# Local attention scores issued in three parts, with the halves of the next key projection between them

## The chip, the cores and the metric

The kernel runs on one core of a Trainium2 chip. The metric is the device time of one execution in microseconds (us). The core has a matrix engine (TensorE, PE in the profile, with its weight loads shown apart as PEld), VectorE (DVE), ScalarE (ACT), GpSimd (POOL) and SyncE (SP), which here issues the DMAs. Each engine works through its own list of instructions in order; semaphores hold an instruction back until work of another engine is done.

## The reference, cut to what matters

The input x is (2, 1024, 128). The result is x plus a causal attention (8 heads, 2 latent key/value groups) plus the output of a stack of six layers, both applied to the layer-normed x. Each of the six layers is a local attention with 16 heads of width 64 and windows of 32 tokens, and then a gated feed-forward part:

```python
x = attn_layer(shift_tokens(x), Wqkv[i], q_scale[i], k_scale[i], Wo[i]) + x
x = ffn_layer(shift_tokens(x), ln_g[i], ln_b[i], W1[i], b1[i], W2[i], b2[i]) + x
# inside attn_layer: q, k l2-normalised, scaled, rotated by position; then for each window of 32 queries
sim  = jnp.einsum('bhwie,bhwje->bhwij', bq, bk2) * QK_SCALE   # 32 queries x 64 keys (the window before and its own)
sim  = jnp.where(mask, -jnp.finfo(sim.dtype).max, sim)
attn = jax.nn.softmax(sim, -1)
out  = jnp.einsum('bhwij,bhwje->bhwie', attn, bv2)
```

The change touches only where the products of `sim` stand in the matrix engine's list.

## The kernel before, in words

The first 250 us or so are the causal attention. Then comes one long software pipeline over 96 tiles of 128 tokens (6 layers x 16 tiles), one step G per tile, about 15 us each. No loop runs on the chip: everything is unrolled, and each engine has its own hand-written order of calls for a step. A tile k passes through the steps as follows.

- Step G = k: TensorE projects the keys of tile k (`project_keys`, `projected`, L1205, six 128x512 products into banks 0 and 1, three for each half of the heads). ScalarE squares them (`square_keys`, L767), VectorE multiplies them by the cosine and the sine tables (`cosine_keys` L1061, `sine_keys` L1066), and GpSimd adds the two parts (L548). At the end of step k+1 TensorE transposes the keys (`transpose_keys`, L1443).
- Step k+1: TensorE projects the queries into the same banks 0 and 1 (`project_queries`, L1205). It may do so only when `sine_keys` has read the keys out of them, which is the semaphore k_s.
- Step k+2: TensorE computes the values (`values_lower`, `values_upper`, L1494) into banks 4 and 5, ScalarE copies them out (L807) and then writes the mask into the same banks (`mask_scores`, L822). The scores (`scores`, L1479) are added onto the mask: 8 head pairs x 4 windows x 2 heads are 64 small products in the program, 128 matmul records in the trace, since each 32-bit product shows as two. The last one raises s_mm.
- s_mm is waited for by VectorE, which takes the row maxima (`maxima`, L1113) and subtracts them (`subtract`, L1119, which raises s_sub), and by GpSimd, which copies the last window of keys for the next tile (`lookback`, L570). The subtraction frees banks 4 and 5 for `values_lower` of the next step. ScalarE takes the exponentials (L840).
- Later steps: denominators (L1101, L1103), scaling on GpSimd (L543), transposes of the probabilities (L1443), the weighted sum (`weigh`, L1518), and once in four tiles the feed-forward products (L1205 again) with their gelus (L873).

The order of TensorE around the change is, in one step: `weigh`, `values_lower`, `project_queries`, the column transpose of the normed rows (L1536), `transpose_queries`, `values_upper`, some feed-forward products, `transpose_probs`, more of these, `scores`, `project_keys`, `transpose_keys`. VectorE's order is: `sum_queries` (L1095), `cosine_queries`, `sine_queries`, `normalise_rows` (L1128), `maxima`, `subtract`, `cosine_keys`, (once a layer the lower part of W1, L1143), `sine_keys`, `sum_keys` (L1089), `attended` (L1108), `denominators`. In GpSimd's order `scale_keys` (L602) and `lookback` (L570) stand ahead of `rotate_queries` (L553), `scale_queries` (L608) and `rotate_keys` (L548).

Of the kernel before, what the change touches and what calls it, by code (L numbers as in the profile page):

```python
# [33 lines left out]
DEPTH, LH, LD, WIN = 6, 16, 64, 32  # L34
HALF = LD // 2
HD = LH * LD
NP = LH // 2
NW = P // WIN
# [60 lines left out]
def build(nc, x, wqT, wkd4, wvd, wkuT, wvuT, wo, wqk, wvo, w1, w2, par, sca, cst_d, tab_d, out):  # L99
    ctx = ExitStack()  # L100
    with ctx:
# [94 lines left out]
        def bk(i):  # L196
            return banks[:, 512 * i:512 * i + 512]
# [41 lines left out]
        def is_tile(G):  # L239
            return 0 <= G <= LAST_TILE  # L240
# [962 lines left out]
        def _(pe):  # L1203
# [78 lines left out]
                ins.then_inc(s["b1_mm"], 1)  # L1282
                freed[7] = ("b1", l + 1)

            def projected(k, z):

                b, i = tile_at(k)
                xH, xL = xsH[:, b, P * i:P * (i + 1)], xsL[:, b, P * i:P * (i + 1)]
                claim(0, 1)
                for h in range(2):  # L1290
                    c0, c1 = 512 * h, 512 * (h + 1)
                    mm(bk(h), xH, qkH[:, z, c0:c1], True, False)
                    mm(bk(h), xH, qkL[:, z, c0:c1], False, False)
                    ins = mm(bk(h), xL, qkH[:, z, c0:c1], False, True)
                return ins

            def project_keys(k):
                if is_tile(k):
                    pe.wait_ge(s["xs_L"], k // 4 + 1)
                    pe.wait_ge(s["wk_L"], k // TILES + 1)  # L1300
                    projected(k, 0).then_inc(s["k_mm"], 1)
                    freed[0] = freed[1] = ("k_s", k + 1)

            def score_row(o, it, h, i):
# [162 lines left out]
                    transposes(prob[:, k % 2, :]).then_inc(s["pt_mm"], 1)  # L1467
                    freed[2] = freed[3] = ("pt_cp", k + 1)

            def scores(k):  # L1470
                if is_tile(k):
                    pe.wait_ge(s["kT_cp"], k + 1)
                    pe.wait_ge(s["qT_cp"], k + 1)
                    pe.wait_ge(s["s_msk"], k + 1)
                    for j in range(NP):
                        for w in range(NW):
                            for o in range(2):
                                r = slice(64 * o, 64 * o + 64)
                                ins = pe.matmul(bk(4 + o)[WIN * w:WIN * (w + 1), 64 * j:64 * (j + 1)],  # L1479
                                                qT[r, j, WIN * w:WIN * (w + 1)], kT[r, j, WIN * w:WIN * w + 64],  # L1480
                                                start=False, stop=True, skip_group_check=True)
                    ins.then_inc(s["s_mm"], 1)
                    freed[4] = freed[5] = ("s_sub", k + 1)

            def values(k, g):

# [99 lines left out]
            for G in range(STEPS):  # L1586
                if G == 1:
                    shifts(0)
                weigh(G - 4)
                values_lower(G - 2)  # L1590
                project_queries(G - 1)
                ln_columns(G - 6)
                transpose_queries(G - 2)
                values_upper(G - 2)
                up_gate(chunk_at(G, 10), 0)
                up_gate(chunk_at(G, 10), 1)
                up_value(chunk_at(G, 11), 0)
                up_value(chunk_at(G, 12), 1)
                next_products_lower(G - 2)
                down(chunk_at(G, 13))  # L1600
                transpose_probs(G - 3)
                up_value(chunk_at(G, 12), 2)
                up_gate(chunk_at(G, 11), 2)
                scores(G - 2)
                next_products_upper(G - 2)
                if G:
                    project_keys(G)
                next_shifts(chunk_at(G, 12))
                layer_columns(chunk_at(G, 13))
                transpose_keys(G - 1)  # L1610
# [55 lines left out]
```

## Time and profile before

| | |
|---|---|
| median of 3 runs | 1748.52 us (1745.69 to 1751.39) |
| the profiled execution | 1745.55 us |
| its span | 1743.9 us, 72603 instructions |
| busy share | PE 93%, DVE 86%, POOL 77%, ACT 76% |
| TensorE's mean granted clock | 0.984 |
| the 95 intervals from the first scores to the last | 252.5 to about 1696 us, 15.2 us each |

The profile's page gives shares over the whole span. TensorE is the busiest engine, yet four engines are all busy for more than three quarters of the time, so that what counts is which wait ends last at each place of a step. The timeline shows this: each row is one instruction or a run of equal ones, with its start, its length, its engine and line, and in square brackets the time that the engine sat idle before it and what ended this. "issue" there is idle time in which the engine waited for nothing that the profile shows. A name such as "banks<-arena" says what is written and read; the local names kT, qT, kc and so on are all parts of the buffer `arena`.

### The profile page before, as it was taken

Reading aid. Unit: us, or ns where it says so; the run is one execution under the profiler, and the core shown is the slowest. Engines: PE = TensorE matmul, PEld = TensorE weight load, DVE = VectorE, ACT = ScalarE, POOL = GpSimd, SP = SyncE. Lnnn points to the kernel's source line nnn. Section 1 sums busy time; section 2 is a strip of 40 time slices with the busy share of each in tenths; the row PEclk is TensorE's granted clock in tenths of the full one; section 3 lists DMA queues with packets and bytes.
Section 4 is the critical chain, followed back from the end, with each engine's and each line's share of the span. In section 5 each row is a group of like instructions: output and inputs, shape, how many; then the busy total and the mean of one; then the engine's idle time right before and its main releaser. Section 6 shows DMA issues by size and latency. Waiting matters only on the chain.

```text
span 1743.9 us, 72603 instructions
## 1 busy us (share of the span) xinstructions
PE 1619.5 (93%) x31192; PEld 1098.7 (63%) x31192; DVE 1495.5 (86%) x1863; ACT 1318.4 (76%) x1934; POOL 1340.6 (77%) x1311
## 2 busy tenths in 40 slices
PE   6999978889999999999998999999999999999995
PEld 4777855556566666665665666666666666666654
DVE  5677857999889998898998888999999988999982
ACT  3788846687787788778777877877887887788773
POOL 2312159888988899988888888899888998888871
PEclk8999989999999999999999999999999999999997
DMA  5221100100001000011000010000010000000001
GB/s 158 67 50 39 38 1 30 35 7 8 15 7 59 6 8 12 16 31 34 8 12 14 8 57 7 7 12 15 7 59 7 12 6 15 8 7 7 8 7 28
DMA packets 47997, 40.61 MB, mean 23 GB/s; under 512 B 33216, under 2 KB 41152, under 8 KB 46016
## 3 DMA queue, kind: packets, MB, share of 16 engines
q1 hardware_dynamic: 47680, 35.98, 7.4%
q8 instruction: 249, 4.08, 0.9%
q14 instruction: 68, 0.56, 0.1%
HBM read 20.22 MB, written 1.05 MB: 12 GB/s over the span
## 4 chain that ended last, share of the span: by engine, by line
PE 51%; DVE 22%; issue 13%; ACT 8%; POOL 6%; DMA 0%; SPq 0%; DVEq 0%; POOLq 0%; ACTq 0%
PE banks L1205 23%; PE banks L1494 9%; PE banks L1443 5%; PE banks L1518 4%; DVE arena L1066 4%; PE banks L1479 4%; PE banks L1335 4%; DVE lnx L1128 3%; DVE small L1095 3%; DVE small L1101 2%; DVE small L1089 2%; DVE small L1113 2%; DVE arena L1061 2%; ACT arena L807 1%; ACT L873 1%
## 5 line engine op out<-in xcount | busy, mean ns | idle before, releaser
L1494 PE MATMUL banks<-M,xs 128*32 128x512 f32 x3072 | 368.0, 596 | 0.6 <-ACT arena L807 0.3
L1061 DVE TENSOR_TENSOR arena<-banks,tabs 128x1024 f32<-128x1024 f32 x192 | 233.8, 1218 | 35.5 <-ACT arena L767 22.4
L548 POOL TENSOR_TENSOR arena<-arena 128x1024 f32<-128x1024 f32 x96 | 229.8, 2393 | 43.7 <-DVE arena L1066 43.3
L807 ACT ACTIVATE arena<-banks 128x1024 f32<-128x1024 f32 x192 | 197.0, 1026 | 68.3 <-PE banks L1494 67.6
L1066 DVE TENSOR_TENSOR arena<-banks,tabs 128x1024 f32<-128x1024 f32 x192 | 233.2, 1215 | 0.0
L553 POOL TENSOR_TENSOR arena<-arena 128x1024 f32<-128x1024 f32 x96 | 228.3, 2378 | 0.0
L543 POOL TENSOR_TENSOR prob<-prob,small 128x1024 f32<-128x1024 f32 x96 | 184.0, 1916 | 30.0 <-DVE small L1103 30.0
L1128 DVE SCALAR_TENSOR_TENSOR lnx<-lns,small 128x128 f32<-128x128 f32 x96 | 175.3, 1826 | 34.2 <-POOL small L596 32.8
L1205 PE MATMUL banks<-qkH,xsH 128*128 128x512 f32 x384 | 173.1, 451 | 32.1 <-DVE arena L1066 29.2
L1518 PE MATMUL banks<-arena 128*32 128x128 f32 x6144 | 190.9, 277 | 5.6 <-ACT arena L873 4.2
L608 POOL TENSOR_TENSOR arena<-arena,small 128x1024 f32<-128x1024 f32 x96 | 182.9, 1906 | 9.8 <-POOL arena L553 0.4
L602 POOL TENSOR_TENSOR arena<-arena,small 128x1024 f32<-128x1024 f32 x96 | 182.9, 1905 | 7.5
L767 ACT ACTIVATE arena<-banks 128x1024 f32<-128x1024 f32 x96 | 98.3, 1024 | 113.6 <-PE banks L1205 113.4
L1479 PE MATMUL banks<-arena 64*32 64x64 f32 x12288 | 147.2, 226 | 32.0 <-issue 17.0
L1518 PEld LDWEIGHTS banks<-arena 128*32 128x32 f32 x6144 | 164.5, 111 | 12.4 <-issue 6.0
L1479 PEld LDWEIGHTS banks<-arena 64*32 64x32 f32 x12288 | 130.1, 105 | 58.4 <-issue 56.8
L1494 PEld LDWEIGHTS banks<-M,xs 128*32 128x32 f32 x3072 | 88.4, 110 | 123.2 <-issue 116.2
L1205 PEld LDWEIGHTS banks<-qkH,xsH 128*128 128x128 f32 x384 | 73.2, 191 | 132.8 <-issue 110.0
L1205 PE MATMUL banks<-qkL,xsH 128*128 128x512 f32 x384 | 153.6, 400 | 2.4 <-issue 2.4
L1205 PE MATMUL banks<-qkH,xsL 128*128 128x512 f32 x384 | 153.7, 400 | 0.0
L778 ACT ACTIVATE arena<-banks 128x1024 f32<-128x1024 f32 x96 | 98.4, 1025 | 72.0 <-PE banks L1205 71.8
L1443 PEld LDWEIGHTS banks<-cst,arena 64*128 64x128 f32 x3072 | 111.5, 139 | 61.8 <-issue 41.9
(134 smaller groups left out, 3645.4 us busy)
## 6 DMA issues: line engine op xcount, KB each, us to landing
qkraw<-in_wqk_dram SPq DMA_DIRECT2D x6, 1024.0 KB, 5.2
arena<-in_wvo_dram SPq DMA_DIRECT2D x5, 1024.0 KB, 5.4
gq<-w1w SPq DMA_DIRECT2D x64, 64.0 KB, 2.0
lns<-Xt SPq DMA_DIRECT2D x96, 32.0 KB
lns<-Xt SPq DMA_DIRECT2D x96, 31.8 KB
xsH<-w1w SPq DMA_DIRECT2D x32, 64.0 KB, 2.0
xsL<-w1w SPq DMA_DIRECT2D x32, 64.0 KB, 2.0
W<-in_w_dram SPq DMA_DIRECT2D x6, 341.0 KB, 3.2
```

The source lines that it names most:

```text
L543: pool.tensor_tensor(p, p, d, ALU.mult).then_inc(s["p_nrm"], 1)
L548: pool.tensor_tensor(kc, kc, ks, ALU.add).then_inc(s["k_add"], 1)
L553: pool.tensor_tensor(qc, qc, qs, ALU.add).then_inc(s["q_add"], 1)
L807: act.activation(vw[:, (2 * k + g) % RV, :], two(V_BANK), ACT.Copy).then_inc(s[f"v_cp{g}"], 1)
L1061: dve.tensor_tensor(heads(c), heads(two(0)), table(k % NT, kind), ALU.mult).then_inc(s[done], 1)
L1066: dve.tensor_tensor(w.rearrange("p (h z k) -> p h z k", h=LH, z=2), swapped(two(0)), table2(k % NT, kind + 1), ALU.mult).then_inc(s[done], 1)
L1128: dve.scalar_tensor_tensor(lnx[:, :], lns[:, k % 2, :], ag[:, k % 2, 0:1], rs[:, 4, 32:33].to_broadcast([P, D]), ALU.subtract, ALU.mult).t ...
L1205: return pe.matmul(o, l, r, start=start, stop=stop)
L1443: ins = pe.transpose(bk(2 + o)[:, 64 * k:64 * (k + 1)], src[r, P * k:P * (k + 1)], ident[r, r])
L1479: ins = pe.matmul(bk(4 + o)[WIN * w:WIN * (w + 1), 64 * j:64 * (j + 1)], qT[r, j, WIN * w:WIN * (w + 1)], kT[r, j, WIN * w:WIN * w + 64], ...
L1494: ins = pe.matmul(bk(V_BANK + z)[WIN * q:WIN * (q + 1), :], xs[:, b, t0:t0 + WIN], M[:, q, :, :].rearrange("p m n -> p (m n)"), start=True ...
L1518: ins = pe.matmul(bk(PV_BANK)[WIN * w:WIN * (w + 1), 0:D], ptile[:, NQ * z + m, WIN * w:WIN * (w + 1)], block_of(k, w - 1 + z)[:, D * m:D ...
```

## The change

The 64 products of `scores` are issued in three parts of 24, 24 and 16 (head pairs 0 to 2, 3 to 5, and 6 and 7). The first three products of `project_keys` stand between the first and the second part, the last three between the second and the third. Where there is no key projection (the last two tiles) the parts stand one after another. The waits ahead of the scores stand ahead of the first part; s_mm is raised by the last product of the third part. `next_products_upper`, which has work once a layer, now stands behind the third part. The operands, the results and all other engines' instructions are the same.

```diff
-            def projected(k, z):
+            def projected(k, z, between=None):
                 ...
                 for h in range(2):
+                    if h and between:
+                        between()
                     c0, c1 = 512 * h, 512 * (h + 1)
                     mm(bk(h), xH, qkH[:, z, c0:c1], True, False)
                     mm(bk(h), xH, qkL[:, z, c0:c1], False, False)
                     ins = mm(bk(h), xL, qkH[:, z, c0:c1], False, True)
...
-                    projected(k, 0).then_inc(s["k_mm"], 1)
+                    projected(k, 0, (lambda: scores_middle(k - 2)) if k >= 2 else None).then_inc(s["k_mm"], 1)
...
+            def scored(k, pairs):
+
+                for j in pairs:
+                    for w in range(NW):
+                        for o in range(2):
+                            r = slice(64 * o, 64 * o + 64)
+                            ins = pe.matmul(bk(4 + o)[WIN * w:WIN * (w + 1), 64 * j:64 * (j + 1)],
+                                            qT[r, j, WIN * w:WIN * (w + 1)], kT[r, j, WIN * w:WIN * w + 64],
+                                            start=False, stop=True, skip_group_check=True)
+                return ins
+
+            def scores_first(k):
                 if is_tile(k):
                     pe.wait_ge(s["kT_cp"], k + 1)
                     pe.wait_ge(s["qT_cp"], k + 1)
                     pe.wait_ge(s["s_msk"], k + 1)
-                    for j in range(NP):
-                        ...
-                    ins.then_inc(s["s_mm"], 1)
+                    scored(k, range(0, 3))
                     freed[4] = freed[5] = ("s_sub", k + 1)
+
+            def scores_middle(k):
+                if is_tile(k):
+                    scored(k, range(3, 6))
+
+            def scores_last(k):
+                if is_tile(k):
+                    if not is_tile(k + 2):
+                        scores_middle(k)
+                    scored(k, range(6, NP)).then_inc(s["s_mm"], 1)
...
-                scores(G - 2)
-                next_products_upper(G - 2)
+                scores_first(G - 2)
                 if G:
                     project_keys(G)
+                scores_last(G - 2)
+                next_products_upper(G - 2)
```

TensorE's list before, from the scores of a tile to the next query projection (L1479 scores, L1205 key projection, L1443 transposes of the keys, L1518 weighted sum, L1494 values, and L1205 at the end the queries; in brackets the semaphores that a row waits for):

```order
L1479 MATMUL banks<-arena 32x64 [waits s_msk,qT_cp,kT_cp]
L1479 MATMUL banks<-arena 32x64 x63
L1205 MATMUL banks<-qkH,xsH 128x512 [waits q_s,wk_L,xs_L]
L1205 MATMUL banks<-qkL,xsH 128x512
L1205 MATMUL banks<-qkH,xsL 128x512
L1205 MATMUL banks<-qkH,xsH 128x512
L1205 MATMUL banks<-qkL,xsH 128x512
L1205 MATMUL banks<-qkH,xsL 128x512
L1443 MATMUL banks<-cst,arena 128x64 [waits pt_cp,k_nrm]
L1443 MATMUL banks<-cst,arena 128x64 x15
```

The same place of the changed kernel's list, where the scores have line L1478 and the transposes L1445:

```order
L1478 MATMUL banks<-arena 32x64 [waits s_msk,qT_cp,kT_cp]
L1478 MATMUL banks<-arena 32x64 x23
L1205 MATMUL banks<-qkH,xsH 128x512 [waits q_s,wk_L,xs_L]
L1205 MATMUL banks<-qkL,xsH 128x512
L1205 MATMUL banks<-qkH,xsL 128x512
L1478 MATMUL banks<-arena 32x64 x24
L1205 MATMUL banks<-qkH,xsH 128x512
L1205 MATMUL banks<-qkL,xsH 128x512
L1205 MATMUL banks<-qkH,xsL 128x512
L1478 MATMUL banks<-arena 32x64 x16
L1445 MATMUL banks<-cst,arena 128x64 [waits pt_cp,k_nrm]
L1445 MATMUL banks<-cst,arena 128x64 x15
```

The last product of the scores stood ahead of all six products of the key projection, and now stands behind all six. The last product of the key projection stood behind 64 products of the scores, and now stands behind 48. VectorE's list around the wait for s_mm is the same in both kernels:

```order
L1128 SCALAR_TENSOR_TENSOR lnx<-lns,small 128x128 [waits lnB_mm,rk]
L1113 TENSOR_REDUCE small<-banks 128x16 [waits s_mm]
L1119 TENSOR_TENSOR prob<-banks,small 128x1024 [waits s_max,pt_mm]
L1061 TENSOR_TENSOR arena<-banks,tabs 128x1024 [waits kT_mm,k_sq,tab]
L1066 TENSOR_TENSOR arena<-banks,tabs 128x1024 [waits k_add,k_sq]
```

The fourth and fifth rows are the cosine and sine products of the keys; they stand behind the row that waits for s_mm.

## Rows read from the trace of the kernel before

**Rows 1.** The profile's page: busy time, and the chain that ended last, by engine.
```profile
PE 1619.5 (93%) x31192; PEld 1098.7 (63%) x31192; DVE 1495.5 (86%) x1863; ACT 1318.4 (76%) x1934; POOL 1340.6 (77%) x1311
...
PE 51%; DVE 22%; issue 13%; ACT 8%; POOL 6%; DMA 0%; SPq 0%; DVEq 0%; POOLq 0%; ACTq 0%
```

**Rows 2.** Waits of TensorE, 260 to 1700 us: total, times, longest, in us.
```profile
PE banks L1205 <- DVE arena L1066: 23.5, 50, 1.8
PE banks L1479 <- issue: 17.0, 14, 2.6
```

**Rows 3.** Waits of VectorE, 260 to 1700 us: total, times, longest, in us.
```profile
DVE small L1113 <- PE banks L1479: 11.5, 11, 2.0
```

**Rows 4.** Timeline of one step, all engines: start, length (us), engine, line, work.
```profile
1261.91 1.47 PE L1479 MATMUL banks<-arena 64*32 64x64 f32 x128
...
1263.32 0.50 PE L1205 MATMUL banks<-qkH,xsH 128*128 128x512 f32 x1
...
1263.65 0.39 PE L1205 MATMUL banks<-qkL,xsH 128*128 128x512 f32 x1
...
1264.43 0.46 POOL L570 COPY arena<-arena 128x256 f32<-128x256 f32 x1
...
1264.56 1.21 DVE L1113 TENSOR_REDUCE small<-banks 128x16 f32<-128x1024 f32 x1
...
1264.90 0.72 PE L1443 MATMUL banks<-cst,arena 64*128 64x64 f32 x16
1265.01 1.03 ACT L767 ACTIVATE arena<-banks 128x1024 f32<-128x1024 f32 x1 [1.92 <-PE banks L1205]
...
1265.87 1.23 DVE L1119 TENSOR_TENSOR prob<-banks,small 128x1024 f32<-128x1024 f32 x1
1267.01 1.22 DVE L1061 TENSOR_TENSOR arena<-banks,tabs 128x1024 f32<-128x1024 f32 x1
...
1267.33 1.93 PE L1494 MATMUL banks<-M,xs 128*32 128x512 f32 x16
...
1267.38 1.90 POOL L608 TENSOR_TENSOR arena<-arena,small 128x1024 f32<-128x1024 f32 x1
...
1268.14 1.22 DVE L1066 TENSOR_TENSOR arena<-banks,tabs 128x1024 f32<-128x1024 f32 x1
...
1269.51 0.47 PE L1205 MATMUL banks<-qkH,xsH 128*128 128x512 f32 x1 [0.25 <-DVE arena L1066]
```

**Rows 5.** The profile's page: the group of all score products (busy, mean ns of one).
```profile
L1479 PE MATMUL banks<-arena 64*32 64x64 f32 x12288 | 147.2, 226 | 32.0 <-issue 17.0
```

**Rows 6.** Timeline of TensorE: scores and the query projection of the next step.
```profile
1277.21 1.48 PE L1479 MATMUL banks<-arena 64*32 64x64 f32 x128
...
1284.90 0.51 PE L1205 MATMUL banks<-qkH,xsH 128*128 128x512 f32 x1
...
1291.55 1.47 PE L1479 MATMUL banks<-arena 64*32 64x64 f32 x128
```

**Rows 7.** Timeline of TensorE: the first and the last of 53 short steps.
```profile
298.57 1.47 PE L1479 MATMUL banks<-arena 64*32 64x64 f32 x128 [1.46 <-ACT banks L822]
...
306.16 0.47 PE L1205 MATMUL banks<-qkH,xsH 128*128 128x512 f32 x1 [0.27 <-DVE arena L1066]
...
1653.23 1.47 PE L1479 MATMUL banks<-arena 64*32 64x64 f32 x128
...
1660.82 0.47 PE L1205 MATMUL banks<-qkH,xsH 128*128 128x512 f32 x1
```

**Rows 8.** Timeline of VectorE: the step in which the lower part of W1 is made.
```profile
1342.81 1.55 DVE L1143 SCALAR_TENSOR_TENSOR w1w<-W,parv,w1w 128x682 fp32r<-128x682 f32 x1
```

**Rows 9.** Timeline of TensorE: scores that stood still in the middle.
```profile
1045.12 0.99 PE L1479 MATMUL banks<-arena 64*32 64x64 f32 x76
1048.73 1.06 PE L1479 MATMUL banks<-arena 64*32 64x64 f32 x52 [2.62 <-issue]
1049.73 0.79 PE L1205 MATMUL banks<-qkH,xsH 128*128 128x512 f32 x1
```

**Rows 10.** The profile's page: the queue that brings instructions (packets, MB, share).
```profile
q8 instruction: 249, 4.08, 0.9%
```

More of the change, by code:

```diff
@@ L1468, in transpose_probs @@
                     freed[2] = freed[3] = ("pt_cp", k + 1)
-            def scores(k):
+            def scored(k, pairs):
[8 more added lines that the diff above has]
+            def scores_first(k):
                 if is_tile(k):
@@ L1474, in scores @@
                     pe.wait_ge(s["s_msk"], k + 1)
-                    for j in range(NP):
[L1476 to L1481, printed above, removed]
-                    ins.then_inc(s["s_mm"], 1)
-                    freed[4] = freed[5] = ("s_sub", k + 1)
+                    scored(k, range(0, 3))
+                    freed[4] = freed[5] = ("s_sub", k + 1)
+            def scores_middle(k):
[6 more added lines that the diff above has]
+                    scored(k, range(6, NP)).then_inc(s["s_mm"], 1)
             def values(k, g):
```

## The prediction, made before the changed kernel had run

> **What bounds the kernel now.** I read the page first. TensorE is busy for 93% of the span and VectorE for 86%, and the chain that ended last spends 51% on TensorE, 22% on VectorE and 13% in time without a visible wait [rows 1]. So TensorE is close to the bound, and part of every step goes through VectorE. Next I read the lists of waits, to see at which places one engine waits for the other. From 260 to 1700 us TensorE waits 50 times, 23.5 us in all, for VectorE's sine product of the keys (L1066) before it projects the queries, and stands still 14 times, 17.0 us in all, in the middle of the scores for nothing that the profile shows [rows 2]. In the other direction VectorE waits for the scores in 11 steps only, 11.5 us in all [rows 3].
>
> Then the timeline of one step, which shows how these two belong together [rows 4]. The reader should follow two paths from the start of the scores, S = 1261.91, to the start of the query projection, Q = 1269.51, and count from S:
> - TensorE's own path: scores, key projection from 1.41, transposes from 2.99, weighted sum, values from 5.42, and Q at 7.60. It has 0.25 us of idle time before Q.
> - VectorE's path: after the normalising of rows (L1128) the maxima start at 2.65, the subtraction at 3.96, the cosine at 5.10, the sine at 6.23, which ends at 7.45, and 0.15 us later Q starts.
> Both paths end together, within a quarter of a microsecond. The scores end at 1.47, and VectorE comes to the maxima only at 2.65: it is 1.18 us late, so that s_mm is not what it waits for. From the start of the maxima to Q it needs 1269.51 - 1264.56 = 4.95 us, with nothing idle in it.
>
> **What the change does to s_mm and k_mm.** It removes and adds no work. First the price of going from scores to a projection. One record of the scores lasts 0.226 us [rows 5], and all of them 1.47, so the last one starts 1.25 after S; the first key product starts at 1.41 [rows 4], 0.16 later. The second starts 0.33 after the first, where the rest follow at (1264.90 - 1263.65)/5 = 0.25 or a little less [rows 4]. So the passage costs about 0.16 + 0.08 = 0.24 us, taken as 0.25. The change makes this passage twice a step instead of once. The trace shows no passage in the middle of a projection, so the bounds are 0 (the weights of the second half are loaded under the scores) and 0.5 (the passage back costs as much again). I take 0.25, by the one passage that the rows show.
> The transposes then start at 2.99 + 0.25 = 3.24, and the last product of the scores stands just ahead of them. It starts a little before, at 3.16 (between 0.01 and 0.16 before, by the spacing of two scores, 1.25/127, and by the passage above), and with its 0.226 ends at 3.38. s_mm is thus late by 3.38 - 1.47 = 1.91 us. k_mm comes only about 0.1 us earlier than before: 32 of the 128 records are no longer ahead of it (32 x 1.47/128 = 0.37), and one more passage (0.25) is. That gives nothing in an ordinary step, because ScalarE's square of the keys starts at 3.10 and is over at 4.13, while the cosine product that waits for it starts at 5.10 [rows 4].
>
> **What stands behind the late s_mm.** VectorE holds four operations behind this wait: maxima, subtraction, cosine, sine. They begin at 3.38 and a few hundredths for the semaphore, say 3.42, instead of 2.65, and Q comes at 3.42 + 4.95 = 8.37; I take 8.40. TensorE's own path would bring it there at 7.35 + 0.25 = 7.60, so it now waits for VectorE, partly before the values (banks 4 and 5 are free when the subtraction ends, at 3.42 + 1265.87 + 1.23 - 1264.56 = 5.96, and TensorE comes there at 5.42 + 0.25 = 5.67) and partly before the queries. From Q to the next S everything hangs on Q (projection, square, copy of the transposed queries, upper values, their copy, the mask) and I leave it unchanged. GpSimd waits for s_mm too, with the copy L570, which comes at 2.52 now and at 3.42 then; the queue behind it is two long operations (L553, L608), which end at 1269.28, 4.85 us after its start. So GpSimd reaches the next addition of keys at 8.27, just when the sine product is over (8.25). That cover is used up to the last tenth. If it falls short, GpSimd's later work comes 0.1 to 0.2 us later in a step, up to 15 us in all, which the range holds.
>
> **The sum.** I read S and Q of 93 steps in TensorE's timeline. In 53 of them Q - S is below 7.86, with a mean of 7.66 (7.59 in the first and the last [rows 7], 7.60 in the example [rows 4], 7.69 in the one behind it [rows 6]). Each of them goes to 8.40:
> - 53 x (8.40 - 7.66) = +39 us.
> - Six steps, one in each layer, have the lower part of W1 (1.55 us, L1143) between the cosine and the sine [rows 8]. It becomes part of the same path: they go from about 8.3 (once 9.2) to about 9.85, +8.5 us.
> - 13 steps in which the scores stand still, or the clock falls after it, have Q - S from 8.3 to 11.4 now. If the standstill goes they take 8.4: -12 us.
> - The other 21 steps are long already for other reasons (a standstill elsewhere, the first and last steps of a layer) and hide the delay: -1 to 0 us.
> - Some standstills stay: +4 us.
> Together about +39 us, to which the last steps, outside the 93, add 1.
>
> **The standstills.** In one step 76 of the records run, then TensorE stands for 2.62 us, and the key product behind it takes 0.79 us [rows 9] instead of 0.50 [rows 4]. Instructions come by a queue of their own, 249 packets with 4.08 MB, 16.4 KB each [rows 10]. Nearly all instructions are TensorE's 2 x 31192 loads and products [rows 1]; 4.08 MB over these are 65 bytes each, so a packet holds about 250 of them, an estimate. One packet takes 0.9% of 16 engines' 1744 us over 249, which is 1.0 us. The scores are 128 loads and 128 products, a packet in 1.47 us, the fastest stretch of the step. My estimate is that the next packet can't come in that time, and that with a projection half (0.95 us) after each 96 instructions it can. Bounds: all 17.0 us go, and with them some 5 us by which the products behind the longest ones are stretched (an estimate: 0.29 us on each of some 17 products), so -22, or none, 0. I take -12 + 4 = -8 net, since part of the gain would be hidden under the longer path, nearer to the first because the standstills lie in the fastest burst.
> The Trainium skill, page "Runtime: NRT & Kernel Launch", section "Instruction fetch mechanics", says that instructions come in blocks of 256 and that their fetch is hidden because the sequencer issues more slowly than the blocks arrive. The block size agrees with the trace; by the second part the standstills have another cause and stay, which is rival B. The 17.0 us that stand in the trace speak against it here.
>
> The profiled execution took 1745.6 us, so the same with the change is 1785.6. The median of the runs is 3.0 above the profiled one, and I predict 1788.
>
> **Rivals.**
> - A, the forecast: s_mm is late by 1.9 us, VectorE's four operations set Q. 1765 to 1808. Chance 0.72. Its lower part is a passage cost of 0: Q at 8.15, -0.25 x 75 = -19 us, 1769.
> - B, the same with standstills that stay where they are (or go into the projection halves): 1788 + 20 = 1808, up to 1815. For it: some stand next to 1 MB loads of weights, which splitting doesn't move. Against it: most don't. Chance 0.17.
> - C, the delay of s_mm is hidden: VectorE comes to the maxima 1.2 us late anyway, and if its path has slack that I don't see, TensorE's own sum remains: two passages, +0.25 x 93 = +23, and -22. 1749. For it: TensorE is the busiest engine. Against it: 50 waits for L1066 in the trace, so no slack. Chance 0.05.
> - D, faster: the place is the score burst, the mechanism is the instruction supply. The standstills go with their low clock, -22 us, the passages cost nothing, and VectorE's late arrival hides s_mm. 1727. It decides if Q - S stays at 7.7. The 0.25 us of idle time before Q, with VectorE as the reason [rows 4], speak against it. Chance 0.06.
>
> A difference of under 0.3% (5 us) can't be told from none here. Slower by more: A and B, 0.89, and I take 0.01 off for their edge: 0.88. Same: C and that edge, 0.06. Faster: D, 0.06. The range for 8 in 10 is A with its bounds and the start of B: 1764 to 1811.
>
> **What would show it.** Right: VectorE's wait for the scores (now L1478) rises from 11 times to nearly all 96, about 100 us in all; the maxima start within 0.1 us of the last score; Q - S is 8.3 to 8.5 in ordinary steps; TensorE waits for the subtraction (L1119) before the values, which it never did, and for L1066 before the queries in most steps; the standstills in L1478 fall well below 17 us. The step from 1261.91 to 1277.21, 15.3 us long [rows 4, 6], would take 16.1. Wrong: if Q - S stays at 7.7 (C or D), if the maxima don't start at s_mm, or if the first product of the second half starts more than 0.3 us or less than 0.1 us after the middle scores.

## The result: 4.5% slower, twice the predicted loss

The changed kernel takes 1831.07 us (median of 6 runs, 1825.78 to 1832.87); the kernel before took 1752.19 in the runs beside it (6 runs, 1745.69 to 1757.31). The ratio is 1.045, with a 95% interval from 1.0425 to 1.0476. The forecast was 1788 in a range of 1764 to 1811: slower was right, the size was not. The profiled execution has a span of 1831.2 us, 87.3 more than the 1743.9 before.

The page of the changed kernel, first the busy times (us and share of the span), then the chain that ended last:

```profile
PE 1685.6 (92%) x31192; PEld 1100.6 (60%) x31192; DVE 1500.1 (82%) x1863; ACT 1327.9 (73%) x1934; POOL 1339.3 (73%) x1311
...
PE 58%; DVE 21%; issue 13%; ACT 5%; POOL 2%; DMA 0%; DVEq 0%; SPq 0%; ACTq 0%; POOLq 0%
```

VectorE, ScalarE and GpSimd do the same work in nearly the same time as before [rows 1] in a longer span. TensorE is shown busy for 66 us more with the same instructions. More than half of that is the scores, whose group has 183.8 us on this page and 147.2 on the page before [rows 5]: the three parts of a step count 0.71 + 0.72 + 0.45 = 1.88 us, the whole counted 1.47. The waits say where the rest of the longer span went. TensorE's, from 260 to 1785 us (total, times, longest):

```profile
PE banks L1205 <- DVE arena L1066: 35.0, 74, 2.1
PE banks L1510 <- DVE prob L1119: 20.7, 63, 2.1
...
PE banks L1445 <- POOL prob L543: 6.4, 11, 0.8
PE banks L1478 <- issue: 3.4, 4, 1.9
PE banks L1445 <- ACT M L826: 3.1, 5, 0.6
```

The wait for the sine product of the keys grew from 50 times and 23.5 us [rows 2]; the wait of the values (L1510) for the subtraction is new; the standstills in the scores fell from 14 and 17.0 us [rows 2] to 4 and 3.4. VectorE's wait for the scores, and then GpSimd's:

```profile
DVE small L1113 <- PE banks L1478: 121.0, 93, 4.0
```

```profile
POOL arena L570 <- PE banks L1478: 108.9, 81, 3.2
POOL arena L567 <- PE banks L1478: 21.9, 11, 2.2
```

VectorE waited for the scores in 11 steps before [rows 3], and now in 93. One ordinary step of the changed kernel, which answers to [rows 4] (start, length, engine, line, work, and in brackets the idle time before it):

```profile
1354.02 0.71 PE L1478 MATMUL banks<-arena 64*32 64x64 f32 x48 [0.15 <-ACT banks L822]
...
1354.63 2.10 DVE L1128 SCALAR_TENSOR_TENSOR lnx<-lns,small 128x128 f32<-128x128 f32 x1 [0.70 <-POOL small L596]
...
1354.66 0.50 PE L1205 MATMUL banks<-qkH,xsH 128*128 128x512 f32 x1
1354.68 1.91 POOL L602 TENSOR_TENSOR arena<-arena,small 128x1024 f32<-128x1024 f32 x1
...
1355.23 0.40 PE L1205 MATMUL banks<-qkH,xsL 128*128 128x512 f32 x1
1355.56 0.72 PE L1478 MATMUL banks<-arena 64*32 64x64 f32 x48
1356.21 0.50 PE L1205 MATMUL banks<-qkH,xsH 128*128 128x512 f32 x1
...
1357.11 0.45 PE L1478 MATMUL banks<-arena 64*32 64x64 f32 x32
...
1357.49 0.71 PE L1445 MATMUL banks<-cst,arena 64*128 64x64 f32 x16
1357.69 1.23 DVE L1113 TENSOR_REDUCE small<-banks 128x16 f32<-128x1024 f32 x1 [0.96 <-PE banks L1478]
1357.72 0.40 POOL L570 COPY arena<-arena 128x256 f32<-128x256 f32 x1 [1.14 <-PE banks L1478]
...
1359.02 1.23 DVE L1119 TENSOR_TENSOR prob<-banks,small 128x1024 f32<-128x1024 f32 x1
1360.16 1.22 DVE L1061 TENSOR_TENSOR arena<-banks,tabs 128x1024 f32<-128x1024 f32 x1
...
1360.39 1.92 PE L1510 MATMUL banks<-M,xs 128*32 128x512 f32 x16 [0.30 <-DVE prob L1119]
...
1361.29 1.22 DVE L1066 TENSOR_TENSOR arena<-banks,tabs 128x1024 f32<-128x1024 f32 x1
...
1362.65 0.47 PE L1205 MATMUL banks<-qkH,xsH 128*128 128x512 f32 x1 [0.34 <-DVE arena L1066]
```

Counted from S = 1354.02, the scores end at 3.54, the maxima start at 3.67, and Q, the start of the query projection, comes at 8.63. Before it was 1.47, 2.65 and 7.60. Both engines, VectorE and GpSimd, stand before the same semaphore for a microsecond.

The rows of L1128 and L602 show something that was overlooked when the slack at the maxima was read: what makes VectorE late there. The normalising row (L1128) is small. Its last four executions in the kernel before, with nothing of GpSimd beside them, take 0.34 to 0.35 us, and it takes 2.1 us here, beside GpSimd's scaling of the keys (L602). In 91 of its 96 executions, in this kernel as in the one before, it lasts 0.14 to 0.19 us longer than its overlap with L602. In the step of [rows 4] this scaling also ends where the maxima start:

```profile
1262.58 1.91 POOL L602 TENSOR_TENSOR arena<-arena,small 128x1024 f32<-128x1024 f32 x1
1263.09 1.55 DVE L1128 SCALAR_TENSOR_TENSOR lnx<-lns,small 128x128 f32<-128x128 f32 x1
```

The slack of 1.18 us thus hung on the place of L602 in GpSimd's list. No run moved L602, so what that would do to the time is not shown.

### The profile page after: what moved, and what is told of

Read it like the earlier page. It is cut to its first block, busy times and chain, and to the rows that moved or that the text cites. A ratio compares the mean times of both kernels' runs of the same rounds, so it can differ in the third digit from the quotient of the medians.

```text
span 1831.2 us, 72603 instructions
## 1 busy us (share of the span) xinstructions
PE 1685.6 (92%) x31192; PEld 1100.6 (60%) x31192; DVE 1500.1 (82%) x1863; ACT 1327.9 (73%) x1934; POOL 1339.3 (73%) x1311
## 4 chain that ended last, share of the span: by engine, by line
PE 58%; DVE 21%; issue 13%; ACT 5%; POOL 2%; DMA 0%; DVEq 0%; SPq 0%; ACTq 0%; POOLq 0%
PE banks L1205 30%; PE banks L1478 9%; PE banks L1510 8%; DVE small L1113 5%; DVE arena L1066 5%; PE banks L1445 4%; PE banks L1337 4%; DVE arena L1061 2%; ACT arena L807 2%; PE banks L1534 2%; ACT banks L822 2%; DVE small L1101 2%; DVE small L1089 2%; DVE arena L1152 1%; DVE prob L1119 1%
## 5 line engine op out<-in xcount | busy, mean ns | idle before, releaser
L1510 PE MATMUL banks<-M,xs 128*32 128x512 f32 x3072 | 371.4, 600 | 21.3 <-DVE prob L1119 20.7
L548 POOL TENSOR_TENSOR arena<-arena 128x1024 f32<-128x1024 f32 x96 | 229.9, 2395 | 21.7 <-DVE arena L1066 18.1
L1066 DVE TENSOR_TENSOR arena<-banks,tabs 128x1024 f32<-128x1024 f32 x192 | 233.2, 1215 | 0.0
L1205 PE MATMUL banks<-qkH,xsH 128*128 128x512 f32 x384 | 182.0, 474 | 44.3 <-DVE arena L1066 40.8
L1113 DVE TENSOR_REDUCE small<-banks 128x16 f32<-128x1024 f32 x96 | 117.6, 1225 | 126.6 <-PE banks L1478 126.6
L1128 DVE SCALAR_TENSOR_TENSOR lnx<-lns,small 128x128 f32<-128x128 f32 x96 | 175.2, 1825 | 38.9 <-POOL small L596 38.6
L1478 PEld LDWEIGHTS banks<-arena 64*32 64x32 f32 x12288 | 138.1, 106 | 111.8 <-issue 110.3
L543 POOL TENSOR_TENSOR prob<-prob,small 128x1024 f32<-128x1024 f32 x96 | 184.1, 1917 | 28.8 <-DVE small L1103 28.8
L1478 PE MATMUL banks<-arena 64*32 64x64 f32 x12288 | 183.8, 224 | 18.2 <-ACT banks L822 12.1
L608 POOL TENSOR_TENSOR arena<-arena,small 128x1024 f32<-128x1024 f32 x96 | 183.0, 1906 | 9.8 <-POOL arena L553 0.4
L602 POOL TENSOR_TENSOR arena<-arena,small 128x1024 f32<-128x1024 f32 x96 | 182.9, 1905 | 7.5
L1510 PEld LDWEIGHTS banks<-M,xs 128*32 128x32 f32 x3072 | 89.0, 110 | 156.4 <-issue 148.6
L840 ACT ACTIVATE prob<-prob 128x1024 f32<-128x1024 f32 x96 | 101.6, 1058 | 95.8 <-DVE prob L1119 95.5
L767 ACT ACTIVATE arena<-banks 128x1024 f32<-128x1024 f32 x96 | 98.3, 1024 | 97.9 <-PE banks L1205 97.5
L1205 PEld LDWEIGHTS banks<-qkH,xsH 128*128 128x128 f32 x384 | 72.9, 190 | 151.3 <-issue 124.2
L1205 PE MATMUL banks<-qkH,xsL 128*128 128x512 f32 x384 | 154.9, 404 | 0.0
```

The source lines that it names most:

```text
L543: pool.tensor_tensor(p, p, d, ALU.mult).then_inc(s["p_nrm"], 1)
L548: pool.tensor_tensor(kc, kc, ks, ALU.add).then_inc(s["k_add"], 1)
L608: pool.tensor_tensor(heads(qc), heads(qc), over(rs[:, 4, LH:2 * LH], LD), ALU.mult).then_inc(s["q_nrm"], 1)
L1066: dve.tensor_tensor(w.rearrange("p (h z k) -> p h z k", h=LH, z=2), swapped(two(0)), table2(k % NT, kind + 1), ALU.mult).then_inc(s[done], 1)
L1113: dve.reduce_max(nmax[:, :], two(4).rearrange("p (h k) -> p h k", h=LH), AXX).then_inc(s["s_max"], 1)
L1205: return pe.matmul(o, l, r, start=start, stop=stop)
```

## The experiments

Each time is a median; each ratio is to the kernel before, timed beside it on the same chip, and has its 95% interval.

### Is it the late semaphore or the added passages?

`keys_first` gives the key projection whole and then the scores whole: s_mm is late, but nothing is split.

```diff
-                scores(G - 2)
-                next_products_upper(G - 2)
                 if G:
                     project_keys(G)
+                scores(G - 2)
+                next_products_upper(G - 2)
```

> The kernel before with one edit: all six key products ahead of all 64 score products, nothing split. s_mm is late by a whole projection, but there is no passage back into a projection. Theory 1 (the late s_mm holds VectorE's four operations, and they set the start Q of the query projection): the scores end 3.1 to 3.3 us after the block of the two begins, Q comes 4.9 to 5.1 us after that, as in the changed kernel, and the time is 1795 to 1820 us. The scores stand whole, so their standstills come back: 10 us or more of unexplained idle time in the scores from 260 us to the end. Theory 2 (not the lateness but the two added passages between scores and projection cost the time): no passage is added, so it is within 5 us of the kernel before, about 1752.

Measured: 1803.27 us, ratio 1.0288 [1.0272, 1.0303]. Theory 1 holds, theory 2 falls: 51 of the 79 us of loss come with the late s_mm alone. In this kernel's timeline:

```profile
1312.57 0.50 PE L1205 MATMUL banks<-qkH,xsH 128*128 128x512 f32 x1
...
1314.16 1.48 PE L1479 MATMUL banks<-arena 64*32 64x64 f32 x128
...
1315.68 1.22 DVE L1113 TENSOR_REDUCE small<-banks 128x16 f32<-128x1024 f32 x1 [1.47 <-PE banks L1479]
```

The scores end 3.07 us after the block of the two begins, in place of 3.54. Of the standstills only 6.8 us (10 times, 260 to 1700 us) came back in the scores, less than expected; 15.4 us (26 times) of the same kind now stood in the weighted sum (L1518), which follows the scores closely here. So these gaps move with the list.

`last_before_half` keeps both passages, but raises s_mm before the last three key products. As a change to the changed kernel:

```diff
             def scores_middle(k):
                 if is_tile(k):
-                    scored(k, range(3, 6))
+                    scored(k, range(3, NP)).then_inc(s["s_mm"], 1)
...
                     if not is_tile(k + 2):
                         scores_middle(k)
-                    scored(k, range(6, NP)).then_inc(s["s_mm"], 1)
```

> The changed kernel with one edit: the third part of the scores follows the second at once and raises s_mm, ahead of the last three key products. Both passages stay, s_mm comes about 0.8 to 1.0 us earlier than in the changed kernel. Theory 1: Q comes 7.8 to 7.9 us after the start of the scores in place of 8.65, and the time falls by about 70 us, to 1755 to 1770. Theory 2 (passages): nothing is gained, 1820 to 1831. The standstills in the scores stay below 8 us by both.

Measured: 1763.19 us, ratio 1.0063 [1.0044, 1.0082]. Theory 1 again: 68 us come back for s_mm 0.96 us earlier. One of its steps:

```profile
1306.85 0.71 PE L1478 MATMUL banks<-arena 64*32 64x64 f32 x48
...
1308.39 1.04 PE L1478 MATMUL banks<-arena 64*32 64x64 f32 x80
1309.36 0.49 PE L1205 MATMUL banks<-qkH,xsH 128*128 128x512 f32 x1
...
1310.26 0.71 PE L1445 MATMUL banks<-cst,arena 64*128 64x64 f32 x16
...
1314.50 0.50 PE L1205 MATMUL banks<-qkH,xsH 128*128 128x512 f32 x1
```

The scores end 2.58 after S, about when VectorE comes to the maxima (2.65 in [rows 4]), and Q comes at 7.65. VectorE's wait for the scores is not all gone: 48 times, 43.7 us in all. The standstills missed: 13.9 us (14 times), not below 8.

With these two there are four kernels that differ in the time at which the scores end. Means over the same 53 ordinary steps, counted from the start of the first score or key product of the block, from the traces:

| kernel | scores end | Q |
|---|---|---|
| before | 1.51 | 7.66 |
| `last_before_half` | 2.63 | 7.86 |
| `keys_first` | 3.11 | 8.20 |
| changed | 3.59 | 8.68 |

The first 1.12 us of delay cost 0.20, since VectorE came late anyway; the next 0.96 cost 0.82.

### Is VectorE's path critical, and since when?

The maxima are taken over a query's own window of 32 keys, half of the elements, in the changed kernel and in the kernel before:

```diff
-dve.reduce_max(nmax[:, :], two(4).rearrange("p (h k) -> p h k", h=LH), AXX).then_inc(s["s_max"], 1)
+dve.reduce_max(nmax[:, :], two(4).rearrange("p (h k) -> p h k", h=LH)[:, :, WIN:2 * WIN], AXX).then_inc(s["s_max"], 1)
```

> The changed kernel, with the row maxima taken over the 32 keys of a query's own window alone (half of the elements are left out of the maximum, not of the softmax). The operation should take some 0.6 us in place of 1.21 and is the first of the four that wait for the scores. Theory 1: each step loses that time in full, 93 x 0.55 = 50 us less, 1775 to 1790. Theory 2 (TensorE's own work sets the step): under 10 us less, above 1820.

> The kernel before with the same half of the maxima left out. Here TensorE's own path ends within 0.25 to 0.4 us of VectorE's, so by theory 1 at most the 23.5 us can go that TensorE waits for the sine product of the keys: 1728 to 1745, a gain of less than half of that in the changed kernel. Theory 2: no change, 1748 to 1755. If the gain is as large as in the changed kernel, VectorE's path set the step before the change as much as after it, and both are wrong on what the change did.

Measured: on the changed kernel 1798.66 us, ratio 1.026 [1.0232, 1.0288], which is 32 us less than with the full maxima. On the kernel before 1750.37 us, ratio 0.9986 [0.9967, 1.0005], no difference that can be told. The same 0.53 us (692 ns for 1225, by the row of L1113) is worth 32 us in one kernel and, by the interval, 6 us at most in the other. So VectorE's path sets the step in the changed kernel, and it hardly did in the kernel before, where it ended level with TensorE's own: there Q - S falls in 26 steps, mostly from 7.59 to 7.23, 8.6 us in all, and TensorE waits for L1066 24 times in place of 50. In the profiled execution longer standstills in the scores (22.3 us for 17.0) and other steps take this back. Both sizes missed: 50 and 7 to 24 us were expected. On the changed kernel part of the rest is seen in the waits:

```profile
PE banks L1205 <- DVE arena L1066: 39.1, 68, 2.6
PE banks L1445 <- POOL prob L543: 19.2, 32, 1.0
```

With VectorE shorter, TensorE waits 19.2 us for GpSimd's scaled probabilities, where it was 6.4 with the full maxima. And the six steps with the row of W1 gain nothing before Q (10.4 us in both), for a reason that comes out two sections below.

### GpSimd's queue behind the same semaphore

GpSimd's copy of the last key window (`lookback`, L570) waits for s_mm. In this experiment it stands behind the addition of the queries, which needs nothing of it:

```diff
-                lookback(G - 1)
                 rotate_queries(G - 1)
+                lookback(G - 1)
```

> The changed kernel, with GpSimd's copy of the last key window (L570, which waits for s_mm) behind the addition of the rotated queries (L553) in its list, in place of ahead of it. Theory G (GpSimd's own queue behind s_mm is a second path of nearly the same length as VectorE's, and costs where GpSimd has extra work in a step): the steps lose the extra 1.0 us between Q and the next S that five of them have, and a few tenths elsewhere, so 1818 to 1828. Theory V (VectorE's path alone): no change, 1828 to 1833.

> The changed kernel with the maxima over half of the elements (half are left out of the maximum) and with GpSimd's copy behind L553. With the short maxima alone only 32 us went where 0.53 us x 93 = 49 were expected, and TensorE then waited 31 times, 18.5 us in all, for GpSimd's scaled probabilities (L543). Theory G: these 17 us come out now, 1779 to 1788. Theory V: something else holds them, 1794 to 1800, no change against the short maxima alone.

Measured: 1810.54 us on the changed kernel, ratio 1.0345 [1.0311, 1.0379], 20.5 us less. With the short maxima as well 1774.02 us, ratio 1.013 [1.0095, 1.0164], 24.6 us less than with these alone. The waits of the second kernel:

```profile
PE banks L1205 <- DVE arena L1066: 23.8, 64, 1.3
...
PE banks L1445 <- POOL prob L543: 4.0, 8, 0.8
```

Theory G holds and was too small: both results are below its range. The time from Q to the next S, summed over 93 steps of the timeline, was 653.7 us in the kernel before, 665.4 in the changed one and 653.4 with the late copy. The forecast had left this stretch unchanged. Nearly all of the 11.7 us stands in nine steps. In five of them, one ahead of each new layer, GpSimd also makes the next layer's key weights (L472, 2.39 us) behind the wait, and TensorE then waits for its scaled probabilities (L543): 5.2 us. In four it is the low clock behind the row of W1: 5.9 us. The L441 (1.30 us) of the step shown above costs nothing there: from Q to the next S it has 7.06 us in both kernels.

The same move on the kernel before:

> The kernel before with GpSimd's copy behind L553 alone. Theory G: GpSimd comes to the copy 1.0 us after the scores have ended, so nothing waits there, and the move frees nothing: within 5 us of 1752. A gain of 20 us as in the changed kernel would say that the place of the copy costs by itself, and not by the late s_mm.

Measured: 1750.23 us, ratio 1.0 [0.9983, 1.0017]. There, in an ordinary step, the copy comes 1.0 us after the scores have ended and waits for nothing (L570 waited for the scores 8 times in all, 8.9 us). It is the late s_mm that made its place cost 20 us.

### The row of W1 and the clock

VectorE makes the lower part of W1 once a layer (L1143), between the cosine and the sine of the keys. Here it stands behind the sine.

```diff
-                next_w1_lower(ahead_at(G, 13))
                 if G:
                     sine_keys(G)
+                next_w1_lower(ahead_at(G, 13))
```

> The changed kernel, with VectorE's lower part of W1 (L1143, 1.86 us, once a layer) behind the sine product of the keys in place of ahead of it. Theory C (in these six steps TensorE stands for 2.1 us ahead of the queries, and in four of them its clock then goes to 1.2 GHz for 3.4 us, which makes the next stretch 1.45 us longer): 6 x 1.8 + 4 x 1.45 = 16 us less, 1811 to 1819, and the low clock in these stretches is gone. Without the clock's part it would be 11 us, 1820. If the W1 row isn't on the path at all: 1831.

Measured: 1819.72 us, ratio 1.0389 [1.036, 1.0418], 11.4 us less. In the changed kernel's timeline of such a step (GpSimd and VectorE, then TensorE):

```profile
1149.02 1.90 POOL L608 TENSOR_TENSOR arena<-arena,small 128x1024 f32<-128x1024 f32 x1
1149.79 1.86 DVE L1143 SCALAR_TENSOR_TENSOR w1w<-W,parv,w1w 128x682 fp32r<-128x682 f32 x1
```

```profile
1152.93 0.47 PE L1205 MATMUL banks<-qkH,xsH 128*128 128x512 f32 x1 [2.04 <-DVE arena L1066]
...
1155.48 1.12 PE L1445 MATMUL banks<-cst,arena 64*128 64x64 f32 x16
1156.53 2.08 PE L1510 MATMUL banks<-M,xs 128*32 128x512 f32 x16
```

TensorE was idle for 2.04 us, and then its 16 transposes took 1.12 us in place of 0.71. The stretches before, in and after this (busy times, the granted clock as a share of 2.4 GHz, DMA share, GB/s) show the clock at 1.2 GHz for most of the middle one:

```profile
1148.90:1152.90 4.00, 1.98 (x28) 0.48 (x17) 4.00 (x4) 2.98 (x3) 1.94 (x2) 1.00 0.00 0
1152.90:1156.90 4.00, 3.97 (x27) 2.80 (x31) 3.54 (x8) 1.53 (x4) 3.65 (x2) 0.57 0.03 7
1156.90:1160.90 4.00, 3.96 (x38) 1.87 (x30) 3.01 (x3) 2.89 (x4) 2.05 (x6) 1.00 0.04 9
```

In four of the six such steps the time from Q to the next S grew by 1.45 to 1.48 us; in the other two TensorE was idle for as long (2.05 and 2.10 us), the clock stayed at 2.4 GHz and nothing was lost there. With the row moved, the clock is not at 1.2 GHz behind Q in any of the six, and Q - S falls by 1.7 to 1.8 us in each. But the time from Q to the next S is then 0.72 to 0.80 us longer in all six than in the kernel before, since the moved row delays the sums behind it, and GpSimd's L548 beside it takes 3.00 us in place of 2.39. The expectation had not counted this. The time of 1819.72 lies just above its range of 1811 to 1819 and is the 1820 that it gave for no part of the clock; the trace shows that the clock's part (5.9 us) was there and that the new delay (4.4 us) nearly made up for it.

The row itself takes 0.92 us in its new place and 1.86 in its old one. What it stands beside decides: in the kernel before, 0.82 us of GpSimd's L608 run beside it and it takes 1.54 or 1.55 in four of six cases; in the changed kernel 1.14 and it takes 1.86; with the short maxima it comes earlier, 1.68 run beside it and it takes 2.40, which is why these steps gained nothing. The short maxima first, then the late copy, where L608 is over before the row begins:

```profile
1125.43 1.91 POOL L608 TENSOR_TENSOR arena<-arena,small 128x1024 f32<-128x1024 f32 x1
1125.65 2.40 DVE L1143 SCALAR_TENSOR_TENSOR w1w<-W,parv,w1w 128x682 fp32r<-128x682 f32 x1
```

```profile
1136.46 1.90 POOL L608 TENSOR_TENSOR arena<-arena,small 128x1024 f32<-128x1024 f32 x1
...
1139.65 0.92 DVE L1143 SCALAR_TENSOR_TENSOR w1w<-W,parv,w1w 128x682 fp32r<-128x682 f32 x1
```

Both moves together on the changed kernel:

> The changed kernel with both list moves. Alone they gave 20.5 and 11.4 us. If they are two separate costs, 1799; if the stretch of low clock behind the W1 row was already freed by GpSimd's earlier copy (6 us counted twice), 1803 to 1807. What is then left over the kernel before, 48 to 56 us, is VectorE's path behind the late s_mm alone (Q 8.65 us after the start of the scores in an ordinary step). If less than 40 us were left, GpSimd's part would be larger than these moves show.

Measured: 1810.62 us, ratio 1.0331 [1.0286, 1.0375]. That is what the late copy alone gave (1810.54), above both expected ranges. The traces say why. The six W1 steps, from S to the next S, stand 17.8 us above the kernel before in the changed kernel, 7.7 with the late copy, 5.7 with the row moved and 5.6 with both. So the late copy alone had freed them of 10 us: with L608 out of the way the row takes 0.92 us, TensorE is idle for 1.1 to 1.2 us in place of 2.04, and the clock stays at 2.4 GHz. Some 2 us were left for the second move, less than can be told here. Half of what the late copy gave was the cost of the W1 row, of which the expectation had seen only the clock's 6 us as counted twice.

### Two tries for a faster kernel

`before_norm_late` moves VectorE's normalising of rows in the kernel before:

```diff
-                normalise_rows(G - 5)
                 maxima(G - 2)
...
                 attended(G - 3)
+                normalise_rows(G - 5)
                 denominators(G - 2)
```

> The kernel before, with VectorE's normalising of rows (L1128) moved from ahead of the maxima to behind the key sums and the attended rows. Theory 1: this row is what VectorE does while the scores run, and what makes it 1.2 us late at the maxima; with it gone s_mm is waited for at once, the four operations start 0.5 to 1.1 us earlier, and TensorE's own path sets Q at 7.35: the waits for L1066 (23.5 us) mostly go, 1730 to 1745. Rival: the moved row delays the denominators and GpSimd's scaling of the probabilities by 1 to 2 us, and TensorE waits there instead: 1752 to 1775.

Measured: 1804.19 us, ratio 1.0304 [1.0272, 1.0337]. It is slower, as the rival had it, but far above its 1752 to 1775, and in the main by another wait than it named:

```profile
PE banks L1536 <- DVE lnx L1128: 48.0, 57, 1.8
PE banks L1205 <- DVE arena L1066: 16.7, 25, 1.7
...
PE banks L1443 <- POOL prob L543: 9.5, 21, 1.5
```

TensorE's column transpose (L1536), which stands right behind the query projection, waits 48.0 us for the moved row. Theory 1's gain is there, and small: over 93 steps the time from S to Q falls from 762 to 748 us. The time from Q to the next S rises from 654 to 724. VectorE came to the maxima in time, and the row was missed elsewhere.

The last two kernels take the two moves to the kernel before, and to `last_before_half`:

> The kernel before (scores whole), with both list moves that helped the changed one: GpSimd's copy L570 behind L553, and VectorE's L1143 behind the sine product of the keys. In the changed kernel the first gave 20.5 us and the second 11. If GpSimd's queue behind s_mm costs the kernel before as well (TensorE waits 5.6 us for L602 and L543 there), up to 6 us go; the W1 row is hidden up to 0.6 us a step, 3 to 4 us go. Theory 1 with G: 1742 to 1749, a small gain, far below the 31 of the changed kernel, because s_mm is early here. If the gain is as large as there, the two waits were not made by the late s_mm.

> Scores in two parts (24, then 40), s_mm ahead of the last three key products, and both list moves. The two parts alone took 1763. TensorE waited there 3.7 us for L543 and 12.3 us for L1066 and stood still 13.9 us in the scores. Theory 1 with G: 1748 to 1758, no better than the kernel before, since two passages cost 0.4 us in each step and the standstills stay. Rival (the split pays once nothing waits for s_mm): below 1742, and below the kernel before with the same two moves.

Measured: 1747.68 us, ratio 0.9999 [0.998, 1.0017], and 1753.01 us, ratio 1.0019 [1.0002, 1.0036]. Both are in their expected ranges, but the small gain expected of the first can't be told. No kernel of the study is faster than the kernel before by more than can be told. With GpSimd's copy out of the way and s_mm 0.96 us earlier than in the changed kernel, the split still gains nothing; VectorE still waits for the scores 47 times, 42.8 us in all. In the rows of `last_before_half` above TensorE's key products and scores take 3.41 us from S to the transposes, against 2.99 before; the standstills in the scores are still 11.8 us in the last kernel.

## Why the prediction was right in direction and wrong in size

**Right: the mechanism of the ordinary step.** The late s_mm holds VectorE's four operations, and they set Q. VectorE waits in 93 steps (forecast: nearly all, about 100 us; 121.0 measured), and TensorE waits for the subtraction before the values, 63 times. k_mm's place gives nothing: in the step shown the square of the keys (L767) ends 1.9 us before the cosine product starts. `keys_first` and `last_before_half` separate this from the passages, and the two kernels with half maxima show it on VectorE itself. Rivals C and D, which needed slack on that path, are out.

**Mis-sized: the ordinary step.** The sum had Q - S at 8.40, and it is 8.63 in the step shown. The same 53 steps went from a mean of 7.66 to 8.68: 54.4 us, where the forecast had 39. S to the end of the scores is 3.54, not 3.38, and the maxima start 0.13 behind it, not 0.04 (and not within the 0.1 that was named as a sign); from there the 4.95 us held (1362.65 - 1357.69 = 4.96). The price of 0.25 us was taken from the one passage from scores into a projection, with nothing for the way back. The rows of the changed step show both ways. From the first key product to the third it is 1355.23 - 1354.66 = 0.57, the same as before (0.33 and about 0.24). From a half's last product to the next scores it is 1355.56 - 1355.23 = 0.33, where two key products follow each other at 0.23 or 0.24. From S to the transposes it is 3.47 us, 0.48 more than before, and not 0.25. The bound of 0.5 was the better value.

**Failed: "from Q to the next S I leave it unchanged", and GpSimd's cover.** The forecast saw GpSimd reach the next addition of keys at 8.27, against 8.25 for the sine product, called the cover used up and put at most 15 us on it, outside the sum. It worked with an ordinary step, and there this held: over the 53 ordinary steps the time from Q to the next S did not change. The steps in which GpSimd has more to do were not worked out. Moving its wait gave 20.5 us, and nothing on the kernel before. By the profiled executions 5.2 us of it stand in the five steps with the next layer's key weights and 10 us in the six W1 steps; the rest lies in single steps, the larger ones with standstills, and is not resolved.

**Failed: the standstill gain.** The standstills in the scores went from 17.0 to 3.4 us, as the estimate of the instruction supply had it, but the time did not fall with them. In the 13 steps in question Q - S fell by 0.3 us altogether, where -12 and +4 stood in the sum, and the time behind Q grew by 2.3. Since Q - S has a floor of 8.6 in every step, and not of 8.40, some 3 us of this are the ordinary term again; and three of the 13 have a standstill or a long wait in the changed kernel too, with Q - S from 10.0 to 11.3. That the gaps come from the supply of instructions was not tested by itself. They lie where many small instructions follow each other and they move with the list (into L1518 in `keys_first`), which speaks for it; that splitting them into 24 and 40 brought only 17.0 down to 13.9 says that the rule is not simply the length of a burst.
The Trainium skill's "Runtime: NRT & Kernel Launch", section "Instruction fetch mechanics", has the fetch hidden. No run here decides it. The traces show 17.0 us in the kernel before and 3.4 in the changed one for the same instructions in another order, so rival B's step, standstills that stay in the scores, did not happen.

**Failed: the W1 steps and the other long steps.** The six W1 steps cost 11.9 us up to Q and 5.9 behind it, in place of 8.5. Two things were missed: the row takes 1.86 us there in place of 1.55, because more of GpSimd's L608 runs beside it, and behind the idle time of 2.04 us the clock was at 1.2 GHz in four of the six. The 21 other long steps were to hide the delay (-1 to 0) and cost 10.3 us before Q and 3.5 behind it. One cause is in the change itself and was not priced at all: `next_products_upper` moved from ahead of the key projection to behind the last scores, just ahead of the transposes, which need the banks that ScalarE has to empty first: 5 waits, 3.1 us, for L826, which the kernel before does not have and `keys_first`, with the same order at this place, has as well. In these five steps Q - S grew by 4.3 us in all.

Altogether, from S to the next S, by the profiled executions (us):

| steps | forecast | measured |
|---|---|---|
| 53 ordinary | +39 | +54.4 |
| 6 with the row of W1 | +8.5 | +17.8 |
| 13 with standstills | -12 + 4 | +2.1 |
| 21 other long ones | -1 to 0 | +13.8 |
| all 93 | +39 | +88.1 |

The whole span grew by 87.3. So the direction came from the mechanism, and the size missed in every row of the table, each time to the same side. The moves show that some 20 us of the loss went through GpSimd's queue; the rest, 59 us by the kernel with its copy moved (1810.54 against 1751.66), stays with VectorE's path and TensorE's passages.

## What to carry to other kernels

Before splitting a block of work to put something between its parts, ask who waits for its last instruction, and list everything that stands behind each such wait on every engine. A consumer that arrives late at a semaphore gives slack of about that size (1.18 us in the ordinary step, none in the 11 steps in which it waited already); beyond it nearly the whole delay is paid, and on each engine that waits. Ask what makes the consumer late: here it was a row of 0.34 us stretched to 1.5 to 2.1 beside another engine's work. A path that "ends level" with the bound has a price in every step that is longer than the ordinary one, and wants its own term in the sum.

## What the runs showed of the hardware that was not expected

Going back and forth between 64-row products with 32-column weights and 128-row products with 128-column weights costs on both sides: 0.34 us to the second product in place of 0.23, 0.33 from the last one to the first small product. Both 24 + 24 + 16 and 24 + 40 added 0.4 to 0.5 us per step to the same work. Behind an idle time of TensorE of 2.04 us its clock was at 1.2 GHz in four steps of six, and 16 transposes took 1.12 us in place of 0.71; in the other two, behind 2.05 and 2.10 us, it was not.

Some rows of VectorE and GpSimd hardly ran side by side. VectorE's L1143 takes 0.92 us without L608 beside it, and 1.54, 1.86 and 2.40 with 0.82, 1.14 and 1.68 us of it; L1128 takes 0.34 alone and 2.1 beside L602. Where L1143 began 0.16 us ahead of L548 it kept its 0.92, and L548 took 3.00 in place of 2.39. The maxima, the subtraction and the products with the tables, which read the banks, took 1.21 to 1.23 us in every kernel with full maxima, beside GpSimd's long rows as well as without them.
